# One product instruction per state in a state space scan on one Trainium2 core

## The reference

```python
xr = x @ w_in + b_in
xc, res = jnp.split(xr, 2, axis=-1)
u = jax.nn.silu(_causal_conv(xc, w_conv, b_conv))
A = -jnp.exp(A_log)
dt, B, C = jnp.split(u @ w_x, [DTR, DTR + N], axis=-1)
delta = jax.nn.softplus(dt @ w_dt)
deltaA = jnp.exp(delta[..., None] * A)
deltaBu = delta[..., None] * B[:, :, None, :] * u[..., None]
# step: h = a * h + bu, along the sequence
y = jnp.einsum('bldn,bln->bld', hs, C) + u * D
return y * jax.nn.silu(res) @ w_out
```

## Time and profile before

| | |
|---|---|
| median of 3 runs | 3209.34 us (3204.06 to 3211.26) |
| profiled execution | 3212.8 us, its span 3210.8 us |
| VectorE busy | 1940.4 us, 60% of the span |
| TensorE matmul busy | 2671.9 us, 83% |
| ScalarE busy | 1290.5 us, 40% |
| GpSimd busy | 1435.8 us, 45% |
| the stage of the change | from about 1535 to 2034 us of the span |

### The profile page before, as it was taken

The page is one execution under the profiler, slowest core; times in us unless marked ns, Lnnn a source line. Parts: engine busy times, 40 slices in busy tenths (PEclk is TensorE's granted clock), DMA queues, the critical chain, the costliest instruction groups (busy, mean ns, idle before and its releaser), DMA issues. The chain is left out here.

```text
span 3210.8 us, 73196 instructions
## 1 busy us (share of the span) xinstructions
PE 2671.9 (83%) x28237; PEld 1889.6 (59%) x28237; DVE 1940.4 (60%) x4348; ACT 1290.5 (40%) x2179; POOL 1435.8 (45%) x1581
## 2 busy tenths in 40 slices
PE   7988939989999889785788887784877999998594
PEld 4655539966776656564233332353446888887593
DVE  4757752137767566532799999536665676665223
ACT  3533434421111044222656655342233656654253
POOL 5646632222212165343787888524462132223355
PEclk9989959989999999798899999896788999999797
DMA  9200015610000100043222222000000000000475
GB/s 329 79 1 2 2 33 173 174 51 3 3 3 3 43 11 12 29 120 106 67 72 69 67 70 71 9 2 1 2 1 11 6 15 12 14 9 14 132 230 158
DMA packets 116937, 177.17 MB, mean 55 GB/s; under 512 B 33265, under 2 KB 78577, under 8 KB 115953
## 3 DMA queue, kind: packets, MB, share of 16 engines
q1 hardware_dynamic: 101648, 155.94, 16.0%
q0 software_dynamic: 7168, 14.78, 1.3%
q10 hardware_dynamic: 7776, 1.77, 0.3%
HBM read 150.01 MB, written 38.40 MB: 59 GB/s over the span
## 5 line engine op out<-in xcount | busy, mean ns | idle before, releaser
L674 POOL TENSOR_SCALAR arena<-arena 128x4 f32<-128x4 f32 x120 | 27.5, 229 | 742.6 <-DVE arena L666 661.2
L2912 POOL TENSOR_TENSOR arena<-arena 128x512 f32<-128x512 f32 x256 | 321.3, 1271 | 70.6 <-DVE arena L3001 63.4
L3001 DVE TENSOR_TENSOR_SCAN arena<-ps,arena 128x512 f32<-128x512 f32 x256 | 314.0, 1227 | 32.0 <-ACT ps L2847 29.4
L2694 PE MATMUL ps<-arena,const_w 128*128 128x512 f32 x512 | 273.4, 619 | 16.2 <-DVE arena L3009 15.0
L163 PEld LDWEIGHTS ps<-L_attn_w,arena 128*128 128x128 f32 x1984 | 240.6, 193 | 55.8 <-issue 38.9
L163 PE MATMUL ps<-L_attn_w,arena 128*128 128x128 f32 x1984 | 257.8, 280 | 9.2 <-ACT arena L2777 4.7
L2847 ACT ACTIVATE ps<-arena,aneg 128x504 f32<-128x504 f32 x256 | 166.6, 677 | 62.1 <-DVE arena L3001 61.3
L1744 PE MATMUL ps<-arena,L_attn_w 128*128 128x512 f32 x384 | 184.5, 617 | 0.9 <-ACT arena L755 0.9
L1812 ACT ACTIVATE arena<-ps,L_attn_w 128x512 f32<-128x512 f32 x64 | 44.0, 687 | 332.7 <-PE ps L1744 332.7
L3009 DVE TENSOR_TENSOR arena<-arena,ps 128x512 f32<-128x512 f32 x256 | 171.9, 672 | 0.0
L435 ACT ACTIVATE arena<-ps 128x1024 f32<-128x1024 f32 x96 | 98.3, 1024 | 152.7 <-PE ps L337 152.7
(11 more groups left out here) (491 smaller groups left out, 6507.9 us busy)
## 6 DMA issues: line engine op xcount, KB each, us to landing
arena<-b_rows SPq DMA_DIRECT2D x128, 256.0 KB
arena<-zone_w SPq DMA_DIRECT2D x54, 512.0 KB, 3.7
arena<-pair_w SPq DMA_DIRECT2D x40, 578.0 KB
pair_in<-pair_free SPq DMA_DIRECT2D x1, 17680.0 KB, 78.8
arena<-rt SPq DMA_DIRECT2D x24, 384.0 KB
arena<-pair_in SPq DMA_DIRECT2D x40, 130.0 KB
arena<-ctx SPq DMA_DIRECT2D x16, 256.0 KB, 5.4
arena<-pair_out SPq DMA_DIRECT2D x16, 256.0 KB, 4.6
```

What stands on the lines that cost most here:

```text
L2694: pe.matmul(acc(c), e.ident, hc(m, c), start=(k == 0), stop=(k == N - 1)).then_inc(s["acc_mm"], 1)
L2912: q.tensor_tensor(bu(m, c), du(g, c), bs(m), ALU.mult).then_inc(s["bu_done"], 1)
L3001: v.tensor_tensor_scan(hs(m, c), at(2 * m + c), bu(m, c), 0.0, ALU.mult, ALU.add).then_inc(s["hs_done"], 1)
```

## The change

`contribute` no longer takes a half: one instruction over 128x1024 elements multiplies both halves of hs(m) by cbank(m), which is repeated for the second half, and raises hc_done by 2. It waits for both scans of its state and both accumulates of state m-2. In VectorE's iteration m it stands behind both scans, for state m-1, so the order becomes scan(m,0), scan(m,1), contribute(m-1). `skipped` moves from ahead of scan(1,0) to behind scan(1,1). The waits in `scan`, `c_row` and `accumulate` are the same lines as before.

```diff
-            def contribute(m, c):
+            def contribute(m):
                 if m >= 0:
-                    v.wait_ge(s["hs_done"], 2 * m + c + 1)
+                    v.wait_ge(s["hs_done"], 2 * m + 2)
                     v.wait_ge(s["c_mm"], m + 1)
                     if m >= 2:
-                        v.wait_ge(s["acc_mm"], 2 * (m - 2) + c + 1)
-                    v.tensor_tensor(hc(m, c), hs(m, c), cbank(m), ALU.mult).then_inc(s["hc_done"], 1)
+                        v.wait_ge(s["acc_mm"], 2 * (m - 2) + 2)
+                    v.tensor_tensor(tiles(both(hc, m), 2), tiles(both(hs, m), 2), repeat(cbank(m), 2), ALU.mult
+                                    ).then_inc(s["hc_done"], 2)
+
+            def both(t, m):
+                return (hs_t if t is hs else hc_t)[:, (m % 2) * 2 * GT:(m % 2 + 1) * 2 * GT]
...
                 g, k = m // N, m % N
-                if k == 1 and g >= 1:
-                    skipped(g - 1)
                 scan(m, 0)
-                contribute(m - 1, 1)
                 if k == 9 and g + 1 < NG:
                     below_high(g + 1)
                 scan(m, 1)
-                contribute(m, 0)
+                if k == 1 and g >= 1:
+                    skipped(g - 1)
+                contribute(m - 1)
                 if g + 2 < NG and k == 7:
                     ln.stats(v, g + 2)
                 if k == 7 and g >= 1:
                     residual(g - 1)
-            contribute(M - 1, 1)
+            contribute(M - 1)
```

## The result

The changed kernel takes 3299.97 us (median of 4, 3294.48 to 3304.02) where the kernel before, over the first series and this one, takes 3209.45 (median of 4, 3204.06 to 3211.26): ratio 1.0295 [1.0282, 1.0307], 90.5 us slower. The forecast was 3294, 3262 to 3318. The profiled execution took 3301.95 us, its span 3300.1.

A forecast was written before the change was run, and what follows sets the result against it. VectorE was taken to set the pace. Stalls from TensorE's late side steps and VectorE's longer sequence summed to 79 us over eight groups, plus 6 for the clock: 85 on 3209, so 3294 us, range 3262 to 3318.

The forecast's parts named there:

- The main term: TensorE's queue: products arrive late, so side steps, ScalarE's copies and decays come late; +9.6 us of stalls per group.
- The side step: TensorE's work for the next group (convolve, channels, step_size, turn), predicted 2.10 us after E, the fused product's end.
- the stalls at scans 3 and 5: VectorE waiting for decays behind the convolve side steps of k=1 and k=3; 1.75 us each.
- scan 7: VectorE waiting for the decay behind the channels side step of k=5; a stall of 0.89 us.
- scan 8: VectorE's wait behind k=6 (channels, two Silu, two table loads); a stall of 3.00 us against 1.41 before.
- Scan 15: VectorE waiting for the decay behind the turn side step of k=13; a stall of 0.38 us.
- The term of VectorE's sequence: VectorE: fused product and the scan waiting on it lengthen a state by 0.11 us (-0.03 to +0.18), +1.7 per group.
- The clock: TensorE falling to 1.2 GHz after idle time: one fall per group, about 1.0 us, six groups; +6 us (0 to 25).
- 1 (TensorE's shift hidden): TensorE's later start is hidden, only VectorE's own sequence counts: +12, 3221 us (3206 to 3232); chance 0.09.
- 3 (faster): VectorE's queue: fixed instruction cost really paid twice, wait free; 3192 us, or 3205 if mostly overlapped; chance 0.03.
- 4 (no change): On VectorE the merged product and the wait cancel and the rest is hidden: 3209 us; chance 0.03.
- 2 (the clock falls at nearly every long wait, 3315 to 3330): TensorE loses its clock at nearly every long wait: 79+25 us and more; chance 0.07.

The follow-up runs named there:

- run 1: The changed kernel with TensorE's side steps (convolve, channels, step_size, turn) put ahead of accumulate(m-1,0); 3211.83 us, ratio 1.0014 to the kernel before.
- run 3: The kernel before, VectorE untouched, with TensorE's accumulate(m-1,0) waiting for both halves' products; 3226.45 us, ratio 1.0071.
- run 5: The changed kernel with c_row's matmul repeated behind the side steps of k = 4, 7, 8, 11 and 12; 3288.57 us, ratio 1.0266.
- run 4: The kernel before with one wait added: scan(m,0) also waits for the product right ahead of it; 3215.62 us, ratio 1.0030.
- run 6: The changed kernel with a third buffer for hs, so a scan waits for the product of m-3; 3292.42 us, ratio 1.0282.
- run 8: Against the kernel before: fused product between the two scans, and TensorE's side steps ahead of the accumulates; 3186.53 us, ratio 0.9948.
- run 7: The kernel before with TensorE's side steps ahead of accumulate(m-1,0), VectorE untouched; 3188.30 us, ratio 0.9958.
- run 9: Against the kernel before: fused product between the two scans, TensorE's order as before; 3240.21 us, ratio 1.0122.
- run 10: The changed kernel with TensorE's side steps ahead of the accumulates and a third buffer for hs; 3198.57 us, ratio 0.9980 to the kernel before.

## Why the prediction was right

**The main term** held, place by place. The side step came at E+2.16 (2.10 predicted), the stalls at scans 3 and 5 are 1.79 and 1.73 (1.75), and with TensorE kept at work scan 7 gives 0.87 (0.89). Run 1 takes the cause away and with it 92 us of stage; run 3 adds a piece of it alone and gets that piece. Its small error is the start of the accumulate, 0.14 behind the product's end instead of 0.06. At scan 8 2.31 us came instead of 3.00, since the longer stall at scan 7 delays VectorE by 1.65 us and TensorE's side step of k=6 only by 0.9 (1870.97, E+2.99 instead of E+2.10). In run 5 it is 2.51, behind 0.47 that VectorE had already waited for TensorE's output in `residual`, together 2.98. Scan 15 got 0.35 and 0.56 in two groups of run 5, where 0.38 was forecast.

**The term of VectorE's sequence** was sized too small. The product lasts 1.195 (1.21 predicted), but the scan starts 1.33 behind its start, not 1.25, just outside the bounds (1.11 to 1.32): a state is 2.25 + 1.33 = 3.58, +0.16 instead of +0.11. The Trainium skill, "VectorE: DVE Perf Modes", in its section on DRAIN, says that a semaphore after an operation costs nothing extra, measured on a chain of copies. For a wait on the instruction right ahead that isn't so here: runs 4 and 6 show 0.12 us behind 512 elements, 0.21 behind 1024. Its formula would give the product 1.22, and 1.195 is near that. In the changed kernel the whole effect hardly shows, since stalls absorb it (11 of 27 us in run 6).

**The clock** was sized too small: 6 us forecast, at least 15 of the stage measured (595.4-579.9). The prediction had one fall in each group at about 1.0 us. It fell four times in the group looked at, twice on the path: at k=5, where it costs 1.67 at scan 7 (2.54-0.87), since accumulate, c_row and accumulate lie on the path and run slowly (1864.46 to 1868.17, 3.71 us, where k=1 takes 2.02), and at k=13, where it costs 0.98 at scan 15 (1.54-0.56). The range allowed for 25.

**The sum.** In run 5 the stage is 579.9-498.0 = 82 us longer than before, which is near the 79 forecast at full clock, though the clock isn't at full there throughout; in the changed kernel it is 97 longer, where 85 were forecast. The time grew by 90.5; the rest of the kernel, which no edit touches, was 8 us shorter in the profiled execution. So the forecast was 12 us short on the stage and only 5.5 on the time, and that difference is luck.

**The rivals.** 1 (TensorE's shift hidden) fell to the timeline and run 1, 3 (faster) and 4 (no change) fell with the result. What 3 rests on is there, but small: with no wait behind it the fused product saves 0.06 us a state (3.36 against 3.42, run 8 against run 7), and run 9, which has that sequence and TensorE's order as before, is still slower. Of 2 (the clock falls at nearly every long wait, 3315 to 3330) the condition largely came true, with four falls in a group, and the price did not, since two of the four lie where nothing on the path waits; its chance of 0.07 was low for that condition.

## What to carry to other kernels

Before two operations of the busiest engine are merged, follow what waits for the first one: its arrival may feed a queue in which the busiest engine's own next input stands, and the slack there (0.6 us here) decides, not the 0.06 us a state saved at the merge (run 8 against run 7). In an in-order queue, put the work that others wait for ahead of an instruction that waits for a late result: this alone gave 12 us on the kernel before (run 7) and 92 us of stage on the changed one (run 1). Once an engine waits, savings on it come back only in part (11 of 27 us in run 6, 0.5 of 7 in run 8, 14.8 of 28 in run 10).

## What the runs showed of the hardware

- A wait on the instruction right ahead on the same engine costs VectorE 0.12 us behind a 512-element product (0.70 against 0.58, run 4) and 0.21 behind one of 1024 (1.33 against 1.12, runs 6 and after). Without the wait the scan starts 0.08 us before the recorded end of the product (run 4, 1674.08 against 1674.16).
- TensorE fell to 1.2 GHz behind idle times of 2.23 us and, in the changed kernel's group from 1844 to 1919, of 2.90, 3.09, 1.65 and 2.76 us (k=5, 8, 11 and 13), and stayed at 2.4 GHz behind 1.80 us at k=1. Small repeated matmuls (42 more in a group) raised the group's granted clock from 0.91 to 0.95 and gave 15 us of the stage back, though they make TensorE busier (63.14 against 56.92 us).
